# First layer of a four-layer graph network: own semaphores for the distance tiles, one PSUM tile in another bank, one matmul earlier on PE

## What is computed

```python
diff = e[:, :, :, None] - offsets          # e = A = adj, 64 offsets
g = jnp.exp(coeff * diff * diff)
h = ssp(jnp.einsum('bijg,fg->bijf', g, W1) + b1)
Wf = jnp.einsum('bijf,gf->bijg', h, W2) + b2
rf = jnp.einsum('bjd,fd->bjf', r, Wa)
Wf = Wf * Am                               # Am = A[:, :, :, None]
y = jnp.einsum('bjf,bijf->bif', rf, Wf * Am)
y = ssp(jnp.einsum('bif,df->bid', y, Wd1) + bd1)
y = jnp.einsum('bid,ed->bie', y, Wd2) + bd2
```

## Time and profile before

| | |
|---|---|
| median of 3 runs | 1743.91 us (1742.11 to 1746.18) |
| profiled execution | 1751.95 us, its span 1750.1 us |
| PE busy | 1289.8 us (74%) |
| DVE busy | 1159.7 us (66%) |
| ACT busy | 828.5 us (47%) |
| POOL busy | 729.0 us (42%) |
| layer 0, steady part | 80 to 867 us |
| end of layer 0 and its flag | 867 to 908 us |
| layers 1 to 3 | 908 to 1750 us |

### The profile page before, as it was taken

How to read it: one execution, slowest core, us unless ns; L and a number is a source line. 1 busy time by engine, 2 the same in 40 slices (tenths; PEclk the granted TensorE clock), 3 DMA queues, 4 the chain that set the end, 5 groups by cost and what they waited for, 6 DMA issues and landing times. The chain is left out here.

```text
span 1750.1 us, 29242 instructions
## 1 busy us (share of the span) xinstructions
PE 1289.8 (74%) x5761; PEld 848.8 (48%) x5792; DVE 1159.7 (66%) x4223; ACT 828.5 (47%) x2049; POOL 729.0 (42%) x1058
## 2 busy tenths in 40 slices
PE   3778778878877887778754755656757788888884
PEld 2444444444444444444433544545546555555564
DVE  4677777777776777777626888888887233333337
ACT  2566666666666665666631322323322233333347
POOL 3454445455544454444533565565655000000007
PEclk9888888898898888888966678778788899999988
DMA  3544544554454454445500000000000000000003
GB/s 86 145 136 130 151 125 126 141 143 126 136 146 125 128 142 132 127 125 140 136 16 7 25 25 12 24 12 24 24 19 13 1 0 0 0 0 0 0 1 97
DMA packets 148629, 128.88 MB, mean 74 GB/s; under 512 B 64963, under 2 KB 127839, under 8 KB 148577
## 3 DMA queue, kind: packets, MB, share of 16 engines
q1 hardware_dynamic: 146852, 127.20, 26.5%
q10 hardware_dynamic: 1725, 1.13, 0.2%
HBM read 123.05 MB, written 5.21 MB: 73 GB/s over the span
## 5 line engine op out<-in xcount | busy, mean ns | idle before, releaser
L501 POOL TENSOR_TENSOR sum<-msg 128x384 f32<-128x384 f32 (+1 forms) x128 | 180.8, 1412 | 407.8 <-DVE msg L861 407.8
L695 PE MATMUL wf<-hid,w2t 128*128 128x384 f32 x512 | 244.6, 609 | 0.0
L729 PE MATMUL rg<-pick,rf 128*128 128x384 f32 x512 | 196.4, 507 | 0.0
L861 DVE SCALAR_TENSOR_TENSOR msg<-wf,b2c,rfe 128x768 f32<-128x768 f32 x128 | 129.8, 1014 | 63.2 <-PE wf L695 62.9
L575 ACT ACTIVATE rfe<-rg 128x768 f32<-128x768 f32 x128 | 103.4, 808 | 139.5 <-PE rg L729 139.5
L835 DVE SCALAR_TENSOR_TENSOR pick<-idx_bc,iota_col,sq_bc 128x768 f32<-128x768 bf16 x128 | 141.5, 1105 | 18.9 <-issue 10.3
L695 PEld LDWEIGHTS wf<-hid,w2t 128*128 128x128 f32 x512 | 106.2, 230 | 82.8 <-issue 58.2
L741 PE MATMUL mb<-wat,xt_w 128*128 128x128 f32 x128 | 33.5, 348 | 152.7 <-ACT over_u L627 146.4
L680 PE MATMUL zb<-gauss,w1t 64*128 64x384 f32 x256 | 133.8, 607 | 12.3 <-ACT gauss L598 9.6
L1592 POOL MEMSET r_minus_half<- 128x4 f32 x1 | 0.1, 101 | 328.0 <-POOLq L1462 328.0
L681 PE MATMUL zb<-gauss,w1t 64*128 64x384 f32 x256 | 133.9, 607 | 0.0
(11 more groups left out here) (266 smaller groups left out, 3454.6 us busy)
## 6 DMA issues: line engine op xcount, KB each, us to landing
sq_bc<-edge_sq SPq DMA_DIRECT2D x128, 384.0 KB, 5.0
val_bc<-edge_val SPq DMA_DIRECT2D x256, 96.0 KB, 3.0
idx_bc<-edge_idx SPq DMA_DIRECT2D x128, 192.0 KB, 4.0
adj_w<-in_adj_rows SPq DMA_DIRECT2D x64, 64.0 KB, 4.4
xt_w<-in_x_cols SPq DMA_DIRECT2D x64, 64.0 KB, 4.1
xin<-in_x_rows SPq DMA_DIRECT2D x32, 128.0 KB, 4.2
m_adj_g<-in_adj_rows SPq DMA_DIRECT2D x16, 256.0 KB, 2.8
m_adjt_g<-in_adj_t SPq DMA_DIRECT2D x16, 256.0 KB, 2.8
```

What stands on the lines that cost most here:

```text
L501: pool.tensor_tensor(sum1[:, 0:wide, :], m[:, 0:wide, :], m[:, wide:2 * wide, :], ALU.add)\
L695: last = pe.matmul(wf[:, half, 0:HALF], w2t[:, :], hid[:, q, half * HALF:(half + 1) * HALF], start=True, stop=True)
L729: last = pe.matmul(rg[:, half, 0:HALF], rf32[:, gn.mod(2), :], picked, start=True, stop=True)
L861: dve.scalar_tensor_tensor(halves(msg[:, q, :]), wf[:, :, 0:HALF], b2c[:, :], halves(rfe[:, q, :]), ALU.add, ALU.mult)\
```

## The change

Three edits, all in layer 0.

The two val_bc transfers of a unit get semaphores of their own, val_in; unit_in counts the other two (32 a unit instead of 64). ACT's dist2 waits for val_in; DVE's pick goes on waiting for unit_in.

The tile p_over_u moves from bank mb to bank ub. Its matmul moves from behind wf to the end of PE's first step, behind p_out, and no longer waits for picks_ready. ACT's copy of it, over_u, moves from the end of the first step to behind rfe in the second. p_rf no longer waits for over_u; instead p_u's first matmul and DVE's xres wait for it.

The prefix count p_start moves to the front of PE's second step, ahead of zb.

```diff
     p_out, p_u = ub[:, 0:P], ub[:, P:2 * P]
-    p_over_u = mb[:, 2 * P:3 * P]
+    p_over_u = ub[:, 2 * P:3 * P]
     p_b2 = mb[:, 203:204]
...
     edges_stored = sem("edges_stored")
+    val_in = [sem(f"val_in{i}") for i in range(UNIT_BUFS)]
     unit_in = [sem(f"unit_in{i}") for i in range(UNIT_BUFS)]
...
-        def unit_count(u, d, q):
+        def unit_count(u, d):
...
             before_pair = per_pair // UNIT_BUFS
-            return u.pair * (64 * before_pair) + 64 * ((u.inner + d) // UNIT_BUFS + 1 + u0 // UNIT_BUFS)
+            return u.pair * (32 * before_pair) + 32 * ((u.inner + d) // UNIT_BUFS + 1 + u0 // UNIT_BUFS)
...
                                  val_src[bass.ds(gi, 1), kk, half * NG:(half + 1) * NG, :]
-                                 .rearrange("a i r -> a (i r)").broadcast_to((NG, HALF))).then_inc(unit_in[q], 16)
+                                 .rearrange("a i r -> a (i r)").broadcast_to((NG, HALF))).then_inc(val_in[q], 16)
                 if dense:
...
                         q = u.mod(UNIT_BUFS, 1)
-                        pool.wait_ge(unit_in[q], unit_count(u, 1, q))
+                        pool.wait_ge(unit_in[q], unit_count(u, 1))
                         pool.tensor_tensor(sq_bc[:, q, :], sq_bc[:, q, :], sq_bc[:, q, :], ALU.mult)\
...
                             .then_inc(s["rfe_ready"], 1)
+                    if not dense and k_in == 1 and g.has(-1):
+                        w(act, "over_u_p", g.at(-1) + 1)
+                        after(act, "u_ready", g, -2, 0)
+                        act.activation(over_u[:, :], p_over_u, ACT.Copy).then_inc(s["over_u_ready"], 1)
                     if not dense and k_in == 0 and g.has(2):
...
                         q = u.mod(UNIT_BUFS, 2)
-                        act.wait_ge(unit_in[q], unit_count(u, 2, q))
+                        act.wait_ge(val_in[q], unit_count(u, 2))
                         after(act, "gauss_ready", u, 1, u0)
...
                             act.activation(logd[:, :], expd[:, :], ACT.Ln, bias=1.0).then_inc(s["log_ready"], 1)
-                    if not dense and k_in == 0 and g.has(-1):
-                        w(act, "over_u_p", g.at(-1) + 1)
-                        after(act, "u_ready", g, -2, 0)
-                        act.activation(over_u[:, :], p_over_u, ACT.Copy).then_inc(s["over_u_ready"], 1)
                     if k_in == 0 and g.has(1):
...
                     q = u.mod(2)
+                    if not dense and k_in == 1 and g.has(3):
+
+                        w(pe, "cnt", g.at(3) + 1)
+                        if g.has(1):
+                            w(pe, "rfhi_ready", g.at(1) + 1)
+                        pe.matmul(p_start, before[:, :], over_cnt[:, :], start=True, stop=True)\
+                            .then_inc(s["start_ready"], 1)
                     if u.has(1):
...
                             .then_inc(s["z_ready"], 1)
-                    if not dense and k_in == 1 and g.has(3):
-
-                        w(pe, "cnt", g.at(3) + 1)
-                        if g.has(1):
-                            w(pe, "rfhi_ready", g.at(1) + 1)
-                        pe.matmul(p_start, before[:, :], over_cnt[:, :], start=True, stop=True)\
-                            .then_inc(s["start_ready"], 1)
                     if u.has(0):
...
                         last.then_inc(s["wf_ready"], 1)
-                    if not dense and k_in == 0 and g.has(-1):
-
-                        w(pe, "msg_ready", u.at(-1) + 1)
-                        if g.has(2):
-                            w(pe, "picks_ready", g.at(2) + 1)
-                        over = msg[:, u.mod(2, -1), :].rearrange("p (i r) -> p r i", r=R)[:, R - 1, :]
-                        pe.matmul(p_over_u, over, wd1t[:, :], start=True, stop=True).then_inc(s["over_u_p"], 1)
                     if k_in == 1 and g.has(-1):
...
                         w(pe, "y_ready", g.at() * (per_graph - 1) + g0)
+                        if not dense:
+                            w(pe, "over_u_ready", g.at(-1) + 1)
                         last = pe.matmul(p_u, wd1t[:, :], y[:, gl, :], start=True, stop=dense)
                         if not dense:
-                            w(pe, "over_u_ready", g.at(-1) + 1)
                             w(pe, "over_t_ready", g.at(-1) + 1)
...
                             w(pe, "picks_ready", g.at(2) + 1)
-                        if not dense and g.has(-1):
-                            w(pe, "over_u_ready", g.at(-1) + 1)
                         after(pe, "rfhi_ready", g, 0, g0)
...
                         pe.matmul(p_out, t_h[:, :], wd2t[:, :], start=True, stop=True).then_inc(s["out_ready"], 1)
+                    if not dense and k_in == 0 and g.has(-1):
+
+                        w(pe, "msg_ready", u.at(-1) + 1)
+                        over = msg[:, u.mod(2, -1), :].rearrange("p (i r) -> p r i", r=R)[:, R - 1, :]
+                        pe.matmul(p_over_u, over, wd1t[:, :], start=True, stop=True).then_inc(s["over_u_p"], 1)
             schedule(pe, body)
...
                         q4 = u.mod(UNIT_BUFS, 1)
-                        dve.wait_ge(unit_in[q4], unit_count(u, 1, q4))
+                        dve.wait_ge(unit_in[q4], unit_count(u, 1))
                         after(dve, "rg_ready", u, -1, u0)
...
                         w(dve, "xb_ready", g.at(-2) + g0 + 1)
+                        if not dense and g.has(-1):
+                            w(dve, "over_u_ready", g.at(-1) + 1)
                         dve.tensor_tensor(xres[:, g.at(-2), :], p_out, xb[:, g.mod(2), :], ALU.add)\
```

## The result

The changed kernel takes 1719.39 us (median of 4 runs, 1717.76 to 1720.27), the kernel before 1745.05 us in the same company (1742.11 to 1747.72): a ratio of 0.9852, 95% interval 0.9834 to 0.9871. The forecast was 1712 us in a range of 1688 to 1735. The profiled execution has a span of 1717.7 us, 32.4 us shorter than that of before. Of several kernels some executions run slower as a whole, at a lower granted clock, and all medians and ratios here are of the others.

A forecast was written before the change was run, and what follows sets the result against it. Bound: SP's round of loads and stores in layer 0, delayed by late squares. Gains of 28 us in the steady part and 4 us at the end, 32 in total, took the median from 1743.9 to 1712 us; range 1688 to 1735.

The forecast's parts named there:

- SP's round: Layer 0: SP loads two units, fetches adjacency and x, stores three tiles, awaits landing; forecast to fall from 13.33 to 12.85 us.
- the 0.81 us: SP's wait for POOL's squares per graph, 47.8 / 59, claimed as the only way the computing engines matter.
- the ring of two graphs: Layer 0's cycle from load through dist2, rf, start, msg, squares and store to load, claimed to make squares late.
- The 5 us: Shortening of layer 0's ring over two graphs, 3.2 + 1.1 + 0.8; squares came at most 3.0 us too late.
- Part (1): ACT's dist2 waits for val_bc alone and may start 3.2 us sooner.
- Part (2): PE's rf no longer waits for over_u: 2.4 us of PE idle per graph freed, 1.1 us in the ring's sum.
- Part (3): Prefix count first in PE's second step: 0.8 us gain where DVE waited, nothing net on a full graph.
- 4 us at the end of the layer: Last graph of layer 0: 3.2 us of dist2's wait for sq_bc and about 1 us of rf's wait go.
- A: Rival: each microsecond by which stores go out sooner is waited at their landing; 1740 us, chance 0.08.
- B: Rival: store landings become worse than the squares' wait they replace; about 1749 us, chance 0.05.
- D: Rival: landings stay at the short value, SP runs at 12.4 us throughout; 1685 us, chance 0.15.
- C: Rival: the new order makes a computing ring the bound, 13.0 to 13.2 us a graph; 1728 us, chance 0.20.

The follow-up runs named there:

- e4: The kernel before, with SP's fetches of adj_w, xt_w and xin issued behind the three stores, ahead of the wait for their landing: ratio 1.0022.
- e1: The kernel before with only the val_in edit, dist2 waiting for val_bc's own semaphore: ratio 0.986 to the kernel before, median 1748.23 us.
- e8: The changed kernel with one semaphore for each of the three stores, edge_sq issued last: ratio 0.9548 to the kernel before, 1668.41 us.
- e3: The changed kernel with SP's fetches of adj_w, xt_w and xin behind the three stores: ratio 0.979 to the kernel before, median 1734.32 us.
- e6: The changed kernel with one more 6 KB load a graph on SP, behind the two units' loads: ratio 0.9964 to the kernel before, 1740.52 us.
- e12: The kernel of e1 with the store semaphores of e8: ratio 0.9631 to the kernel before, 1708.64 us.
- e11: The kernel of e8 with the fetches of adj_w, xt_w and xin behind the stores: ratio 0.9418 to the kernel before, 1670.40 us.
- e7: The changed kernel with one more 384 KB load a graph on SP, behind the two units' loads: ratio 1.0297 to the kernel before, 1801.53 us.
- e9: The changed kernel with the prefix count back behind zb: ratio 0.9871 to the kernel before, median 1752.2 us.
- e10: The changed kernel with p_over_u back in its old bank and place: ratio 0.9883 to the kernel before, median 1751.7 us.

## Why the prediction was right, and where it was not

*What bounds.* Right in its main point: SP's wait for squares fell to nothing, and SP's round sets the pace in all 59 graphs. One sentence went too far, that the computing engines matter only through the 0.81 us a graph in which SP is seen waiting for squares: e4 showed the kernel before held by the ring of two graphs. The forecast did not suffer by it, as the round without any late squares had been taken from the 29 graphs that had none.

*The three edits.* The 5 us by which the ring was to get shorter were more than needed. Part (1), val_in, 3.2 us, was enough alone (e1). The 3.0 us that it took for val_bc were read from a semaphore shared with idx_bc and sq_bc (see e8); with one of its own val_bc stands at 3.2, so little hung on it. Part (2) freed PE's 2.4 us as said, and in the steady part they bought nothing; the 1.1 us that the sum gives it are worked out from no row, and what was seen of them directly is 0.4 to 1.0 us between the last graph's two dist2. Part (3) did bring the count before DVE asked for it, 96.5 us down to 0.5, where the forecast had "halved". Its price was set a little low: the count and its wait for rf were to delay z by 0.4 to 0.7 us, and PE's wait for rf alone is 34.7 / 59 = 0.6 us a graph, beside the count's own 0.38. L802, now L800, stood at a median of 295 ns and at most 1134 ns, with a mean of 566 ns where it was 534:

```profile
L800 DVE TENSOR_SCALAR slot_from<-iota_row,found 128x128 f32<-128x128 f32 x58 | 32.8, 566 | 2.1
```

So the collision with POOL that the Trainium skill (SBUF — State Buffer, "Who interferes with whom") led me to weigh grew, from 14 of 64 graphs at 1.1 us to 20 of 64. The trace agrees: each of the 20 starts 0.94 to 0.98 us after one of POOL's 2.0 us sums of msg and ends within 0.1 us of it. It cost nothing here, as SP sets the pace and DVE has time. "It has hardly waited for them so far", of DVE's pick, was true of before and no longer: 49.8 us in 40 graphs, also without cost.

*SP's round.* 12.85 us was forecast, 12.94 measured. The longer landing, 4.28 us against 3.87, was expected, 4.2 to 4.8, and took back about half of the 0.81 us. This was the term that decided the size. It came right because it was read from the undisturbed graphs and not from the difference 13.33 - 0.81, which would have given 12.52.

*The ends.* 4 us at the end of the layer were 6.7: the first dist2 came 3.9 us sooner (3.2 forecast), the second gained 0.9 more (about 1 forecast, for rf), and for the other 1.9 us no row gives a cause. The first graphs, costed at nothing, gave 2.6. Together with the steady part, 28 forecast and 23.0 measured, the profile's difference is 32.4 us, as against 32 forecast. That the sum is right to half a microsecond is luck: two errors of 5 us cancel. Clearing the extra semaphores, put at under 0.5 us, shows nowhere, as all from the next layer on takes 842 us in both.

*From the profile to the median.* Here is the term that was mis-sized. The profiled execution of before was 8 us above its median and I took all 32 us off the median. The profiled time came out as forecast, 1720 against 1719.5, and that of after lies at its median. The medians differ by 25.7 us, so the forecast of 1712 was 7.4 us low. It may be that part of the slowness of that one execution of before was the very loss that the change takes away; there is only one profile of before, and this is not shown.

*The rivals.* A (the landing takes all of it back) happened by half in the steady part, B and D did not. C did not: SP never waited for a computing engine. Rival A's mechanism, for which the Trainium skill was named (DMA: Bandwidth & Descriptors, "Queues, rings and completion order": a completion lands only after every earlier write of the same DMA engine), is what e3 shows in part: the stores go out 1.5 us sooner and the last lands 1.0 us later after its issue. By that rule alone, with the loads still on their way, e3 would have gained nothing and e6's issue time cost nothing; they gave 0.45 us a graph and cost 23 us, so the rule is a part of the truth and the measurement decides.

*The working.* The range around 12.85 us does not follow from its own bounds: 13.0 and 12.6 us a graph with the 4 us of the end give 1720 and 1697, not 1722 and 1701. Rival D's own time, 1685, lies outside the range that was to hold most of it. And the chances of a slower kernel, 0.05 in B and 0.03 in C, add up to 0.08, not 0.06. None of this moved the forecast.

## What to carry to other kernels

Find the ring that an in-order queue makes with its own transfers, and read the length of its undisturbed rounds from the trace: that length, not the idle time removed, bounds what edits elsewhere can give, and edits that cure the same lateness don't add up. Give each consumer a semaphore for just the transfer that it reads, and do it first on the side that sets the pace; here that was worth 49 us on the stores after 26 to 29 us on the loads. Don't read single landings out of a group of transfers that share a semaphore. And when the profiled execution lies off the median, say so in the range, as here 7 us hung on it.

## What the hardware showed that I had not expected

Stores of 3 or 6 KB issued behind some 1.5 MB of loads are not done as much sooner as they are issued sooner: issued 1.5 us earlier, the last of three took 6.2 us instead of 5.2 (e1 to e3), and edge_val with a semaphore of its own 6.6 instead of 5.5 (e12 to e11, on one chip). Another 378 KB ahead of the stores cost 1.0 us a graph (e6 to e7).

And chips differ in just this stage. The spacing of graphs in which nothing but the landing was waited for was 12.9 us on the two chips where the kernel before takes 1745 us and 13.4 us (e1, e9, e10) where it takes 1776, with the wait on edge_idx at 4.2 to 4.3 us and at 4.7. From the first transfer of the second layer on, all fourteen profiled executions take 838 to 845 us. So most of the 30 us between the chips lies in the first layer.
